# A transformer layer on one core: the attention scores take scaled 16-bit pairs instead of 32-bit pairs, and the first query heads are made around the last feed-forward stage

## Time and profile before

| what | value |
|---|---|
| median of 3 runs | 2282.2 us (2280.94 to 2282.47) |
| the profiled execution, its time | 2282.42 us |
| its span, first to last instruction | 2280.6 us |
| mean granted TensorE clock | 0.999 of full |
| busy: PE, PEld, DVE | 2238.7 us, 1461.6 us, 1574.2 us |
| busy: ACT, POOL | 1108.8 us, 974.3 us |
| keys stage, to the end of the last down product | 541.2 us |
| heads stage | from there to 2280.6 us |

### The profile page before, as it was taken

The page is one execution under the profiler, slowest core; times in us unless marked ns, Lnnn a source line. Parts: engine busy times, 40 slices in busy tenths (PEclk is TensorE's granted clock), DMA queues, the critical chain, the costliest instruction groups (busy, mean ns, idle before and its releaser), DMA issues.

```text
span 2280.6 us, 33617 instructions
## 1 busy us (share of the span) xinstructions
PE 2238.7 (98%) x11776; PEld 1461.6 (64%) x11776; DVE 1574.2 (69%) x3680; ACT 1108.8 (49%) x2184; POOL 974.3 (43%) x808
## 2 busy tenths in 40 slices
PE   8999999998999999999999999999999999999998
PEld 6566675754666666666666666666666666666655
DVE  6666555546777777777777777777777777777765
ACT  3423425244555555555555555555455555555544
POOL 4001020203545455545454554555454545454542
PEclk9999999999999999999999999999999999999999
DMA  5857677596110202020211132220202020202000
GB/s 209 310 155 268 187 224 269 182 337 224 28 61 24 65 23 67 19 69 16 70 37 53 51 98 64 72 61 24 65 20 68 22 65 20 70 23 67 15 27 20
DMA packets 88198, 213.59 MB, mean 94 GB/s; under 512 B 9312, under 2 KB 25952, under 8 KB 81376
## 3 DMA queue, kind: packets, MB, share of 16 engines
q1 hardware_dynamic: 85920, 207.27, 28.5%
q10 hardware_dynamic: 2112, 4.19, 0.5%
HBM read 156.89 MB, written 54.53 MB: 93 GB/s over the span
## 4 chain that ended last, share of the span: by engine, by line
PE 90%; DVE 4%; issue 3%; ACT 2%; POOL 1%; DMA 0%; SPq 0%; DVEq 0%; ACTq 0%; POOLq 0%
PE ob L1341 16%; PE scores L1315 16%; PE qb L1295 13%; PE ob L1352 13%; PE ptb L1327 11%; PE ring L1068 8%; PE ring L1048 6%; PE down L1077 4%; PE ring L1103 2%; ACT short_prob L1184 1%; DVE acc L1266 1%; DVE q_sin L1243 1%; ACT oT L1201 1%; DVE q_cos L1245 1%; DVE q_sin L1244 0%
## 5 line engine op out<-in xcount | busy, mean ns | idle before, releaser
L1198 ACT ACTIVATE pT<-ptb 128x512 f16<-128x512 f32 x576 | 333.9, 591 | 422.7 <-PE ptb L1327 422.4
L1249 DVE SCALAR_TENSOR_TENSOR pT<-ptb,pT 128x512 f16<-128x512 f32 x576 | 390.6, 688 | 81.4 <-ACT pT L1198 76.6
L1341 PE MATMUL ob<-pT,v 128*128 128x512 f16 x1728 | 439.4, 380 | 0.1
L1315 PE MATMUL scores<-kT,late_qT 128*128 128x384 f32 (+3 forms) x1536 | 365.9, 373 | 9.7 <-DVE nmax L1228 8.7
L1163 POOL TENSOR_TENSOR long_prob<-long_prob,rinv 128x384 f32<-128x384 f32 (+3 forms) x256 | 304.2, 1201 | 156.3 <-DVE rinv L1273 155.9
L1169 POOL TENSOR_TENSOR q_cos<-q_cos,q_sin 128x512 f32<-128x512 f32 x124 | 157.5, 1270 | 480.1 <-DVE q_cos L1245 480.1
L1352 PE MATMUL ob<-wo,oT 128*128 128x512 f16 x1536 | 353.6, 380 | 3.5 <-DVE oT L1253 3.5
L1163 POOL TENSOR_TENSOR short_prob<-short_prob,rinv 128x512 f32<-128x512 f32 (+3 forms) x256 | 277.6, 1095 | 180.5 <-DVE rinv L1273 178.5
L1295 PE MATMUL qb<-xT,wq 128*128 128x512 f16 x1488 | 349.3, 379 | 0.0
L1315 PEld LDWEIGHTS scores<-kT,late_qT 128*128 128x128 f32 x1536 | 265.0, 189 | 44.9 <-POOL late_qT L1173 13.4
L1184 ACT ACTIVATE long_prob<-long_prob,nmax 128x384 f32<-128x384 f32 (+3 forms) x256 | 204.7, 800 | 167.6 <-DVE nmax L1228 165.2
(11 more groups left out here) (117 smaller groups left out, 2732.6 us busy)
## 6 DMA issues: line engine op xcount, KB each, us to landing
wq<-w_halves SPq DMA_DIRECT2D x126, 256.0 KB, 3.1
ff_raw<-in_ffw SPq DMA_DIRECT2D x56, 384.0 KB, 5.4
k_parts<-stage SPq DMA_DIRECT2D x128, 128.0 KB, 2.5
w_fetch<-in_wqo SPq DMA_DIRECT2D x16, 1024.0 KB, 5.6
w_fetch<-in_wqo SPq DMA_DIRECT2D x32, 512.0 KB, 4.6
w_halves<-w_parts SPq DMA_DIRECT2D x32, 512.0 KB, 3.1
kT<-k_parts SPq DMA_DIRECT2D x32, 512.0 KB, 5.7
wo<-w_halves SPq DMA_DIRECT2D x16, 1024.0 KB, 4.9
```

Source lines behind the costliest of these rows:

```text
L1198: nc.scalar.activation(pT[:, t % 4, HI], ptb[t % 2][:], ACT.Copy, scale=P_SCALE).then_inc(pT_hi, 1)
L1249: nc.vector.scalar_tensor_tensor(pT[:, t % 4, LO], ptb[t % 2][:], P_SCALE, pT[:, t % 4, HI], ALU.mult, ALU.subtract).then_inc(pT_split, 1)
L1315: mm = nc.tensor.matmul(sc[:, c * 512:c * 512 + cols], q[:, x, i % AHEAD * P:i % AHEAD * P + P], kT[e % 2][:, y, c * cols:(c + 1) * cols], ...
L1341: mm = nc.tensor.matmul(ob[:], v16[e % 2][:, x, j], pT[:, t % 4, y], start=(j == 0 and (x, y) == (HI, HI)), stop=(is_last(kind, n, j) and ...
```

## The change

Four things change.

1. **Keys.** ACT copies each key group out unsplit, DVE takes its largest magnitude (`turned_top`, `keys_top`) instead of a low part, and half as many bytes are stored. The largest of all is gathered (`top_of_keys`, `store_top`, `load_top`, `weight_scales(KEY)`). In the heads stage the keys of one head (512 KB) are loaded into `k32`, scaled and split into 16-bit pairs there, in two halves (`key_hi` on ACT, `key_lo` on DVE). The halves of the next head are placed at the fourth and fifth unit of each key head, those of the values, which are now split in two halves too, at the sixth and seventh (`K_UNITS`, `V_UNITS`), each behind the unit's last scores.
2. **Queries.** q pairs are 16-bit floats; the tables hold a factor 1/16384, and the scale of the scores is applied where DVE reads them, as a value per partition (`score_scale`) in place of the constant -1.
3. **Order at the border.** Q 0 to Q 3 are made before the last chunk's feed-forward stage, into the ring banks, Q 4 ahead of its last down product and Q 5 behind it; Q 6 moves one step forward. The loads, rotations and splits that belong to them move along.
4. **Waits.** Scores 0 and 1 wait for the down banks that they overwrite and those before them, and only scores 2 for all.

```diff
-OPENING = [("Q", 0, 0), ("Q", 1, 0), ("Q", 2, 0), ("S", 0, 0), ("Q", 3, 0), ("S", 0, 1), ("Q", 4, 0),
-           ("S", 0, 2), ("S", 0, 3), ("Q", 5, 0)]
+FIRST = AHEAD + 1
+OPENING = [("Q", 5, 0), ("S", 0, 0), ("S", 0, 1), ("S", 0, 2), ("S", 0, 3)]
...
-            if kind == "Q" and k < EARLY:
+            if kind == "Q" and k <= EARLY:
+                if k == 1:
+                    step.append((0.0, 0, len(PLACES), (kind, n + 1, 0)))
                 continue
...
+    ge, pos = n // TB + 1, n % TB
+    if kind == "S" and j == GRP - 1 and ge < B * KVH:
+        for units, hi, lo in ((K_UNITS, "KH", "KL"), (V_UNITS, "VH", "VL")):
+            if pos in units:
+                half = units.index(pos)
+                return [("act", hi, ge, half, 0.6, 0.1), ("dve", lo, ge, half, 0.95, 0.1)]
     return []
...
-        late_qT = sb("late_qT", 67 * KB, [P, GRP, 2, 512], F32R)
-        spare_turn = sb("spare_turn", 79 * KB, [P, 2, 512])
+        late_qT = sb("late_qT", 155 * KB, [P, GRP, 2, 512], F16)
...
-        kT = [sb(f"kT{e}", (115 + 72 * e) * KB, [P, 2, S], F32R) for e in range(2)]
+        kT = [sb(f"kT{e}", (115 + 4 * e) * KB, [P, 2, S], F16) for e in range(2)]
+        k32 = sb("k32", 99 * KB, [P, S])
...
         def load_k(sp, ge):
+            wait(sp, k_split, 2 * ge)
+            sp.dma_start(k32[:].rearrange("p (x t) -> p x t", x=S // CHUNK),
+                         scr["k"][ge % KVH, :, ge // KVH * 2:ge // KVH * 2 + 2]).then_inc(k_loaded, 16)
+
+        def key_hi(act, ge, h):
+            act.wait_ge(k_loaded, 16 * ge + 16)
+            if ge == 0:
+                act.wait_ge(w_scale_ready, 9)
             if ge >= 2:
-                sp.wait_ge(s_done, (ge - 1) * TB * GRP)
-            for x in range(S // CHUNK):
-                sp.dma_start(kT[ge % 2][:, :, x * CHUNK:(x + 1) * CHUNK].bitcast(F32),
-                             scr["k"][ge % KVH, :, ge // KVH * 2 + x]).then_inc(k_loaded[ge % 2], 16)
+                act.wait_ge(s_done, (ge - 1) * TB * GRP)
+            half = slice(h * S // 2, (h + 1) * S // 2)
+            nc.scalar.activation(kT[ge % 2][:, HI, half], k32[:, half], ACT.Copy, scale=w_scale[:, KEY:KEY + 1])\
+                .then_inc(k_hi, 1)
...
+        def key_lo(dve, ge, h):
+            dve.wait_ge(k_hi, 2 * ge + h + 1)
+            half = slice(h * S // 2, (h + 1) * S // 2)
+            nc.vector.scalar_tensor_tensor(kT[ge % 2][:, LO, half], k32[:, half], w_scale[:, KEY:KEY + 1],
+                                           kT[ge % 2][:, HI, half], ALU.mult, ALU.subtract).then_inc(k_split, 1)
+
...
-            if n < AHEAD + EARLY:
-                return first_qb[n % AHEAD]
-            return qb
+            return ring[n] if n < AHEAD else ob if n == AHEAD + 1 else qb
...
+        def early_queries(sp):
+            for p in range(2):
+                sp.wait_ge(w_kept[p], kept_by(CHUNKS - 1))
+            load_wq(sp, 0)
+            load_wq(sp, 1)
+            for h in range(2):
+                sp.dma_start(opening_wq[:, h].rearrange("p x k d -> p (x k d)"),
+                             scr["w"][QUERY, 0, :, 2 + h].rearrange("p x d -> p (x d)")).then_inc(opening_loaded, 16)
...
+            elif m == 11:
+                for x in range(2):
...
+                for n in range(AHEAD, AHEAD + 2):
+                    load_wq(sp, n)
...
+                    if last and n == G_V + 1:
+                        early_queries(sp)
+                    if last and n == G_V + 3:
+                        store_top(KEY)
+                    if last and n == G_V + 7:
+                        load_top(KEY)
...
-            wait(pool, tab2, 16)
-            wait(pool, w_scale_ready, 4)
-            nc.gpsimd.tensor_scalar(qtab[:], qtab[:], q_unscale[:, 0:1], None, ALU.mult).then_inc(qtab_scaled, 1)
+            add_turned(pool, 0)
+            for n in range(1, FIRST):
+                add_turned(pool, n)
+                query_lo(pool, n - 1)
+            query_lo(pool, FIRST - 1)
...
+                if c == CHUNKS - 1:
+                    for n in range(AHEAD - 1):
+                        query_hi(act, n)
                 for m in range(MB):
                     gate(c, m, m % 2)
+                    if c == CHUNKS - 1 and m == 0:
+                        query_hi(act, AHEAD - 1)
...
+                    if c == CHUNKS - 1:
+                        if m in (7, 8):
+                            key_hi(act, 0, m - 7)
+                        if m in (10, 11):
+                            value_hi(act, 0, m - 10)
+                        if m == MB - 1:
+                            query_hi(act, AHEAD)
...
-                    dst = xT[:, :, n - G_XT] if n < G_CT else cT[:, :, n - G_CT] if n < G_KR else stage[:, n % RING]
-                    split_lo(c, n, dst[:, HI], dst[:, LO])
+                    if n >= G_KN:
+                        keys_top(c, n)
+                    else:
+                        dst = xT[:, :, n - G_XT] if n < G_CT else cT[:, :, n - G_CT]
+                        split_lo(c, n, dst[:, HI], dst[:, LO])
...
-            def keys_lo(c, i):
-                s = (G_KR + i) % RING
...
+            def turned_top(c, i):
+
+                wait(dve, k_copied, c * TURNS + i + 1)
+                nc.vector.tensor_reduce(k_tops[:, c * KVH + i:c * KVH + i + 1], k_cos[:, i % 2], AX.X, ALU.max,
+                                        apply_absolute_value=True).then_inc(k_topped, 1)
...
+                    if c == CHUNKS - 1:
+                        if m == 2:
+                            weight_scales(KEY)
+                        if m == 4:
+                            top_of_all()
+                        if m in (8, 9):
+                            key_lo(dve, 0, m - 8)
+                        if m == 10:
+                            value_scales()
+                        if m in (11, 12):
+                            value_lo(dve, 0, m - 11)
...
             for c in range(CHUNKS):
                 projections(c)
+                if c == CHUNKS - 1:
+                    dve.wait_ge(tab2, 16)
+                    for n in range(AHEAD):
+                        rotate(dve, n)
                 ffn(c)
+            dve.wait_ge(q_split, 1)
+            rotate(dve, AHEAD)
             finish_ffn(CHUNKS - 1)
...
                 for side, done in ((0, gate_done), (1, up_done)):
-                    if first:
+                    if first and c == CHUNKS - 1:
+                        wait(pe, q_read, 2 * side + o + 1)
+                    elif first:
                         wait(pe, emptied, c * GROUPS + GROUPS - RING + 2 * side + o + 1)
...
+            def first_query(n):
+                x = n // AHEAD
+                pe.wait_ge(x_ready[x], 16)
+                if n in (2, 3):
+                    pe.wait_ge(opening_loaded, 32)
+                else:
+                    pe.wait_ge(wq_loaded[n % 2], n // 2 * 16 + 16)
+                w_q = opening_wq[:, n - 2] if n in (2, 3) else wq[:, n % 2]
+                if n < AHEAD:
+                    wait(pe, emptied, (CHUNKS - 1) * GROUPS + GROUPS - RING + n + 1)
+                else:
+                    wait(pe, h_ready, CHUNKS * MB - 1)
...
+                if c == CHUNKS - 1:
+                    for n in range(AHEAD):
+                        first_query(n)
                 gate_up(c, 0, 0, first=True)
...
                     project_down(c, m2 * 2 + 2, 0)
+                if c == CHUNKS - 1:
+                    first_query(AHEAD)
                 project_down(c, MB - 1, 1, last=True)
...
                     if j == 0 and n % TB == 0:
-                        pe.wait_ge(k_loaded[e % 2], e // 2 * 32 + 32)
+                        pe.wait_ge(k_split, 2 * e + 2)
                     if n % AHEAD == 0:
                         pe.wait_ge(q_split, query_of(n, j) + 1)
-                    if hd == 0:
+                    if hd < 2:
+                        pe.wait_ge(ff_copied, CHUNKS * CT - 3 + 2 * hd)
+                    elif hd == 2:
                         pe.wait_ge(ff_copied, CHUNKS * CT)
                     if hd > 1:
```

More of the change, by code:

```diff
@@ L251, in orders @@
     done, taken, tiles = {}, {e: [] for e in engines}, []
+    for n in range(FIRST):
+        done["dve", "Q", n, 0] = done["pool", "QL", n, 0] = 0.0
     pe_free, at, calendar, serial = 0.0, 0, [(0.0, 0, "pe", None)], itertools.count(1)
@@ L280, in orders @@
             note(pe_free, "pe", None)
-            for chain in (followers(*event), values_split(*event)):
+            for chain in (followers(*event), pieces_split(*event)):
                 if chain:
@@ L447, in program @@
         acc_ready = [sem(f"acc_ready{i}") for i in range(TB)]
-        k_loaded = [sem(f"k_loaded{e}") for e in range(2)]
+        k_loaded = sem("k_loaded")
+        k_hi = sem("k_hi")
+        k_split = sem("k_split")
         v_loaded = sem("v_loaded")
@@ L539, in turning, with rotate, add_turned, query_hi @@
             return q_cos[:], q_sin[:]
+        def rotate(dve, n):
```

(33 more changed lines are left out.)

209 lines of the change are left out of this document (99 added, 110 removed).

## The result

| | before | after |
|---|---|---|
| median of 4 runs each | 2282.1 us | 2259.7 us (2257.4 to 2261.3) |
| ratio, 95% interval | | 0.990 (0.9885 to 0.9919) |
| the profiled execution | 2282.4 us | 2258.3 us |

The change is faster, by 22 us, where 48 were forecast, with 2254 as the upper end of the range. The sign was right, the size and the range were wrong.

What follows compares the result with a forecast made beforehand. The prediction took PE's queue, busy 98% of the span, as the bound. Its terms -35, -8, 0 and -6, with +1 for new waits, gave -48 from 2282.4 us: 2234 us, range 2221 to 2254.

Steps and rivals of the forecast that it cites:

- Term 1: Score matmuls in the heads stage: 16-bit pairs instead of 32-bit make each one cheaper, -35 us, range 28 to 40.
- Term 2: Fifth unit's 320-column scores: moving the value split takes away 8 of 9.7 us idle time, from 3 to 11.
- Term 3: DVE's added load from slower maxima and split halves: hidden by PE's own work, 0 us.
- the 1 us for new waits: Allowance in the sum for waits that surface when PE is faster: +1 us.
- Rival A: Scores: 16-bit ones are no faster, only the gains at the fifth unit and border remain, 2268 us; chance 0.05.
- the straight line: Rule for 32-bit score prices at widths without a row: interpolate between the read widths; 10 ns gain taken at 256 columns.
- the upper bound of 42: Largest gain from 16-bit scores: 17 ns for each of 1920 matmuls and 47 at 128 columns, 42 us.
- Term 4: Border between feed-forward and heads stages: the new order loses less PE time, -6 us, from 2 to 10.
- The sign given for such a case: Border loads: a load landing late would show as idle time ahead of Q 0; the loads were costed at nothing.
- Rival B: Narrow units: DVE becomes the bound, 12 us of PE's gain and half of Term 2 return, 2250 us; chance 0.2.
- Rival C: DVE's order: each of 60 halves delays a maximum PE needs by 0.9 us, slower at 2295 us; chance 0.02.

Runs made afterwards that it cites:

- experiment 1: Changed kernel with the load of Wq for query head 6 issued before SP's wait for the last down product: 2250.7 us.
- experiment 2: Changed kernel with the key halves at the first and second unit of each key head instead of the fourth and fifth: 2250.5 us.
- experiment 4: Changed kernel with keys and queries split into 32-bit pairs again, the rest of the change kept: 2287.7 us.
- experiment 3: Changed kernel with the constant -1 in place of the factor per partition, scores not scaled back: 2254.4 us.
- experiment 9: experiment 6 with the load of k 1 issued right behind Q 6's load, ahead of the end of the last down product: 2241.4 us.
- experiment 8: experiment 6 with the fourth score product placed behind the PV product in the one-block step: 2261.6 us.
- experiment 5: experiment 1 with the eight loads of acc, wo 1 and k 1 issued behind SP's wait for the feed-forward result's store: 2248.3 us.
- experiment 6: Changed kernel with the edits of experiment 1, experiment 2 and experiment 5 together: 2252.8 us.
- experiment 7: experiment 1 with scores 0 and 1 waiting for all four copies of the down banks, as before the change: 2249.6 us.
- experiment 10: The changed kernel as it is, run again on the same chip as experiment 9: 2259.9 us.

## Why the prediction was wrong, step by step

Against the sum of the prediction (-48) the profiled execution shows -24.1. Term 1 gave 4 us more than it said, the border 10.6 less and the waits in the units 17.3 less (10.3 more where terms 2 and 3 and the 1 us for new waits came to 7 less).

- **Term 1 (-35): right in mechanism, mis-sized by its 128-column part.** Forecast 5.9 us at 128 columns, from a guessed 72 ns; measured 57 ns and a gain of 48 ns each: 192 x 48 = 9.2. The wide ones came about as forecast: 0.64 us for three of 512 columns. By these parts the sum is 38 to 39. Rival A is excluded. Two slips did no harm: at 256 columns the straight line that the term names gives some 23 ns and not 10 (the starts in the traces show 10, so this number was right by luck), and the upper bound of 42 counts 1920 wide matmuls, where there are 2112; with them it is 45. The Trainium skill, "TensorE: Matmul & The Clock Gate", section "Back-to-back issue gap", gives 81 ns at 128 columns; these runs do not bear it out, and the form columns/2.4 + 3 ns, which was only one bound of the range, holds down to 128 columns.
- **Term 4 (-6): the failed step is "four loads ... I cost these at nothing".** I looked at the loads of Q 0 to 5 and not at that of Q 6, which I had moved ahead of the first T in my own sum ("Q 6 then takes until 12.8"). Its load stands in SP's queue behind the wait for the store. The PE side of the working was exact: with the load moved, 12.74 and 12.80 us for 12.8. The load cost 11.8 us at the border and 8 to 9 us of the time (experiment 1), since it hid the wait of ACT's first pT on the same store. The sign given for such a case, idle time ahead of Q 0, looked at the wrong Q.
- **Term 2 (-8): the failed step is "that is level, or nearly so ... I take 8 of the 9.7 us away".** A step's sum is no chain. (Its 0.9 us for scores are at the 16-bit price already, though rival B calls the 8.3 us the work before that gain; it would be 8.6.) The half lies between a maximum and a reciprocal, with POOL's division of 2.46 us for two heads behind it and PE waiting for the last. The old waits at the 320-column scores (11.1 us by the prices) went; 7.0 came back at the first T that follows the fifth unit's scores, 7.0 at its fourth scores and 3.6 in the one-block step. The second is at the place of the old wait: the low part of Q 7 came only 0.5 us before the maximum that the prediction read as the cause, so the 9.7 us of idle time could not fall by 8. The prediction costed POOL as covered. Experiment 2 shows what the place of the halves is worth: 5.7 us go when they stand in the first and second unit. The other two waits stay in it (6.3 us of idle time at the fourth scores); experiment 4 shows that up to 8 us of the waits hang on the faster matmuls.
- **Term 3 (0): failed by 3 us.** 61 ns per maximum were foreseen and taken as covered. They are not everywhere (experiment 3).
- **Rival B** had the right kind of loss (PE gains in narrow units, DVE and POOL chains don't), with a chance of 0.2 and a size of 16 us against the forecast, which is near the 17 that terms 2 and 3 missed. Its reason, that DVE's work in the step exceeds PE's, is not what the runs show: experiment 2 leaves DVE the same work and has 5.7 us less of waits. So the nearness of the size is luck. Rival C's mechanism acted in one of the four places of a half, at 0.47 us instead of 0.9.
- **The range** reached to 2254, B's case, and held no case in which a queue at the border is late. With experiment 9's version, where that is mended and the halves are moved, the time is 2241, 7 us over the forecast: term 2 still gives nothing (waits from 600 us on are 24.8 us, 22.7 before), which costs 12 with the waits nearer to the border, and terms 1 and 4 give 4 and 1 more than forecast.

What stays open: why the store at the border lands in 11.4 us in one execution and in 13.3 in another, with the same loads beside it, and so how much of experiment 2's shorter wait there is its own. And the wait for Q 7's low part on POOL, 7 us, is left; no run shows a cure, and experiment 8 was the wrong one.

## What to carry to other kernels

When a step on the critical engine is moved earlier, follow its load through the issuing queue to the last wait ahead of it; here one 256 KB load behind one `wait` cost 8 to 9 us, more than the 7 that the new order at the border gives without it. A gain in matmul time is given back wherever a chain through the other engines ended the step, so add up the chain (split, reciprocal, division, transpose) and not each engine's work. And a wait that is mended uncovers the next one: test mends together, and look at what each queue holds in the version they make.

## What the runs showed of the hardware

- In the changed kernel a 16-bit matmul with its own weight load costs, by the starts, 56 to 57 ns at 128 columns, 109 at 256, 136 at 320, 189 at 448 and 213 to 216 at 512: columns/2.4 plus 2 to 4 ns. The 32-bit one costs 48 ns more at 128 (experiment 4).
- A factor per partition instead of a constant costs DVE's custom maximum 60 to 62 ns at every width from 128 to 1024 columns (287 to 347 ns, 820 to 881, 1220 to 1281; experiment 3 against the changed kernel).
- A store of 1 MB lands in 4.3 us when 3.5 MB of loads are issued behind it (experiments 5, 6, 8 and 9) and in 11.4 to 13.3 with these loads beside it (the changed kernel and experiments 1 to 4, 7 and 10).
- In the changed kernel PE idled for 9.1 us and the granted clock fell to 0.50 meanwhile; the Q after it took 5.30 us for 2.75, and from 577.3 us on the clock was full again.
